# Second attention of a two-layer block: softmax weights turned one step later, ahead of the norm in VectorE's step

## The chip, the cores and the metric

One Trainium2 chip, one core. The metric is the device time of one execution in microseconds (us), the median of several runs. Engines: PE is TensorE, DVE is VectorE, ACT is ScalarE, POOL is GpSimd, and SP issues most of the DMAs.

## The reference

Two layers over x of shape (8, 512, 256), 4096 tokens of width 256. Each layer modulates a layer norm, adds a gated attention, norms again, and adds a gated mixture of experts. The change lies in the attention of the second layer, where each token attends over its own 16 heads, not over other tokens:

```python
h = _layernorm(x) * (1 + ca) + sa
Q, K, V = (x @ Wq.T), (x @ Wk.T), (x @ Wv.T)      # each reshaped to (b, s, 16 heads, 16)
scores = jnp.einsum('bshd,bstd->bsht', Q, K) / math.sqrt(hd)
attn = jax.nn.softmax(scores, axis=-1)            # 16 x 16 for every token
out = jnp.einsum('bsht,bstd->bshd', attn, V).reshape(b, s, dm)
x = x + ga * (out @ Wfc.T)
h = _layernorm(x) * (1 + cb) + sb                 # then the second layer's experts: logits = h @ Wg, ...
```

## The kernel before, in words

The kernel is written engine by engine, with explicit semaphores (`c_["name"]`, counted up by one for each tile). The second attention works on 32 tiles (NT) of 128 tokens; four tiles (TB) form a batch. It is a software pipeline: `tile_steps` runs a step counter s, and in step s every stage with lag LAG handles tile t = s - LAG, in the order of the list that the engine hands over. No scheduler moves anything: the list is the engine's program order, and an engine that waits holds up all that stands behind.

The way of one tile, with line, engine and lag before the change:

- L1576 PE turns the normed rows (2), ACT shifts them (L1502), L1585 PE makes values (3), L1509 ACT keeps them, SP stores and reloads them (L1342, L1352).
- L1596 PE makes queries and keys (6), L1515 ACT keeps them; after every fourth tile SP moves the keys with four DMAs (`turn_k`, L1361).
- L1652 PE `scores` (10), into PSUM banks 0 to 3, which are not doubled: the scores of a tile wait until ACT has copied those of the tile before (`compact`, L1523, semaphore `comp`).
- L1396 POOL `mask_other` (11), L1429 DVE `max_scores` (11), L1401 POOL `sub_max` (11), L1530 ACT `exps` (12), L1433 and L1434 DVE `sum_exp` (12), L1406 POOL `normalize_exp` (13), L1443 DVE `turn_exp` (13): four block transposes that turn the weights into `ebd`. All of them work in place on the buffer `sc`.
- L1631 PE `weigh` (14), L1536 ACT keeps the result. After every fourth tile L1607 PE `project` (15), into the same PSUM banks as the scores, and L1453 DVE `gate_attention` (15), for which the next scores wait.
- L1412 POOL `add_attention` (19), L1459 and L1460 DVE `stats_sum` (19), L1492 and L1494 ACT `rstd2` (19), L1469 and L1470 DVE `norm2` (20), L1616 PE `turn_h` (20), L1542 ACT `keep_h1T` (20), L1640 PE `logits` (20), L1546 ACT `keep_logits` (20).

Every fourth step is a step with a projection; PE and ACT use a second list in it. In ACT's ordinary list the copy of the scores is in two halves, and the second half, which alone counts `comp` up, stands behind `keep_h1T`; in the list of a step with a projection the whole copy stands first:

```python
tile_steps([(LAG_MX, compact((0, 1), False)), (LAG_N, shift_h), (LAG_V, keep_v), (LAG_EX, exps), (LAG_H, keep_h1T),
            (LAG_MX, compact((2, 3), True)), (LAG_QK, keep_qk), ...],
           [(LAG_MX, compact((0, 1, 2, 3), True)), ...])
```

The last four tiles' norms run after the loop (`LAST`), and in the two last steps with weights PE runs 12 filler matmuls (`hold_clock`, L277).

Of the kernel before, what the change touches and what calls it, by code (L numbers as in the profile page):

```python
# [61 lines left out]
def two_layer_kernel(nc, a):  # L62
    ctx = ExitStack()
    with ctx:
# [1203 lines left out]
        zqk = [cv(P * H).rearrange("p (t h) -> p t h", h=H) for _ in range(2)]  # L1268
        zk = [cv(P * H).rearrange("p (t h) -> p t h", h=H) for _ in range(2)]
        ebd = [cv(GR * P).rearrange("p (g n) -> p g n", g=GR) for _ in range(2)]  # L1270
        sc = [cv(GR * 32).rearrange("p (g n) -> p g n", n=32) for _ in range(3)]
        oT = cv(HH * P).rearrange("p (j t) -> p j t", j=HH)
        h1 = [rows[:, i * D:(i + 1) * D] for i in range(2 + TB)]
        yb = cv(TB * D).rearrange("p (k d) -> p k d", d=D)
# [24 lines left out]
        v_d = nc.dram_tensor("v_turn", [NT, P, D], F32).ap()  # L1299

        LAG_N, LAG_V, LAG_VST, LAG_QK, LAG_VLD, LAG_S = 2, 3, 4, 6, 7, 10
        LAG_MX, LAG_EX, LAG_ET, LAG_PV, LAG_Y = 11, 12, 13, 14, 15
        LAG_XLD, LAG_ROW, LAG_X, LAG_H = 14, 16, 19, 20

        def tile_steps(stages, project_steps=None):

# [19 lines left out]
        with nc.Block() as block:  # L1326
# [59 lines left out]
            @block.gpsimd  # L1386
            def _(eng):
                attn0_gpsimd(eng)
                f0_gpsimd(eng)
                eng.memset(ebd[0], 0.0)  # L1390
                eng.memset(ebd[1], 0.0).then_inc(s_ebz, 1)

                def mask_other(t):
                    eng.wait_ge(c_["comp"], t + 1)
                    s3 = sc[t % 3]
                    eng.tensor_tensor(s3, s3, bc_mid(pair_mask, GR), ALU.add).then_inc(c_["msk"], 1)  # L1396

                def sub_max(t):
                    eng.wait_ge(c_["mx"], t + 1)
                    s3 = sc[t % 3]  # L1400
                    eng.tensor_tensor(s3, s3, bc_last(mx1[t % 2], 32), ALU.subtract).then_inc(c_["sub"], 1)  # L1401

                def normalize_exp(t):
                    eng.wait_ge(c_["sm"], t + 1)
                    s3 = sc[t % 3]
                    eng.tensor_tensor(s3, s3, bc_last(rs1[t % 2], 32), ALU.mult).then_inc(c_["mul"], 1)  # L1406

                def add_attention(t):
                    b, k = t // TB, t % TB
                    eng.wait_ge(c_["ya"], b + 1)  # L1410
                    eng.wait_ge(s_x1[b % 2], 16 * (b // 2 + 1))
                    eng.tensor_tensor(xr[b % 3][:, k, :], xr[b % 3][:, k, :], yb[:, k, :], ALU.add).then_inc(c_["xa"], 1)  # L1412
                tile_steps([(LAG_ET, normalize_exp), (LAG_X, add_attention), (LAG_MX, mask_other), (LAG_MX, sub_max)])
                for t in LAST:
                    add_attention(t)

            @block.vector
            def _(eng):
                attn0_vector(eng)
                plan0_vector(eng)  # L1420
                f0_vector(eng)
                ch = Chain(eng, "s_vc")
                for v in vp[0:2]:
                    eng.memset(v, 0.0)
                eng.memset(vp[2], 0.0).then_inc(s_vz, 1)

                def max_scores(t):
                    eng.wait_ge(c_["msk"], t + 1)
                    eng.tensor_reduce(mx1[t % 2], sc[t % 3], AX.X, ALU.max).then_inc(c_["mx"], 1)  # L1429

                def sum_exp(t):
                    eng.wait_ge(c_["ex"], t + 1)
                    ch.do(eng.tensor_reduce(rs1[t % 2], sc[t % 3], AX.X, ALU.add))  # L1433
                    eng.reciprocal(rs1[t % 2], rs1[t % 2]).then_inc(c_["sm"], 1)  # L1434

                def turn_exp(t):
                    eng.wait_ge(c_["mul"], t + 1)
                    if t < 2:
                        eng.wait_ge(s_ebz, 1)
                    wait_some(eng, c_["pv"], t - 1)  # L1440
                    for q in range(4):
                        rows_q = slice(32 * q, 32 * q + 32)
                        last = eng.transpose(ebd[t % 2][rows_q, :, 32 * q:32 * q + 32], sc[t % 3][rows_q])  # L1443
                    last.then_inc(c_["et"], 1)

                def gate_attention(t):
                    b = t // TB
                    if t % TB == TB - 1:
                        eng.wait_ge(c_["y"], b + 1)
                        eng.wait_ge(s_m3[b % 2], 48 * (b // 2 + 1))  # L1450
                        wait_some(eng, c_["xa"], TB * b)
                        for k in range(TB):
                            last = eng.tensor_tensor(yb[:, k, :], b_y[k], mod3[b % 2][:, 0, :], ALU.mult)  # L1453
                        last.then_inc(c_["ya"], 1)

                def stats_sum(t):
                    eng.wait_ge(c_["xa"], t + 1)
                    ln = one_of(ln2, t)
                    ch.do(eng.bn_stats(ln[0], xr[t // TB % 3][:, t % TB, :]))  # L1459
                    eng.bn_aggr(ln[1], ln[0]).then_inc(c_["mv2"], 1)  # L1460

                def norm2(t):
                    m3 = mod3[t // TB % 2]
                    h, (_, mean, rstd) = one_of(h1, t), one_of(ln2, t)
                    eng.wait_ge(c_["rs2"], t + 1)
                    if t < FIRST_LAST:
                        wait_some(eng, c_["tH"], t - 1)
                        wait_some(eng, s_hst[t % 2], t // 2, 16)
                    ch.do(eng.scalar_tensor_tensor(h, xr[t // TB % 3][:, t % TB, :], mean[:, 0:1], m3[:, 1, :], ALU.subtract, ALU.mult))  # L1469
                    eng.scalar_tensor_tensor(h, h, rstd, m3[:, 2, :], ALU.mult, ALU.add).then_inc(c_["h"], 1)  # L1470
                tile_steps([(LAG_H, norm2), (LAG_ET, turn_exp), (LAG_X, stats_sum), (LAG_MX, max_scores), (LAG_EX, sum_exp),
                            (LAG_Y, gate_attention)])
                norm2(FIRST_LAST - 1)
                stats_sum(FIRST_LAST)
                for t in LAST:
                    if t + 1 < NT:
                        stats_sum(t + 1)
                    norm2(t)

            @block.scalar  # L1480
            def _(eng):
# [35 lines left out]
                def compact(quads, done):  # L1517
                    def stage(t):
                        eng.wait_ge(c_["ss"], t + 1)
                        wait_some(eng, c_["et"], t - 2)  # L1520
                        for q in quads:
                            rows_q = slice(32 * q, 32 * q + 32)
                            last = eng.activation(sc[t % 3][rows_q], b_s[rows_q, :, 32 * q:32 * q + 32], ACT.Copy)  # L1523
                        if done:
                            last.then_inc(c_["comp"], 1)
                    return stage

                def exps(t):
                    eng.wait_ge(c_["sub"], t + 1)
                    eng.activation(sc[t % 3], sc[t % 3], ACT.Exp, scale=HD ** -0.5).then_inc(c_["ex"], 1)  # L1530

                def keep_oT(t):
                    p = t % TB
# [334 lines left out]
```

## Time and profile before

| | before |
|---|---|
| median of 3 runs | 1058.15 us (1058.12 to 1059.05) |
| the profiled execution's own time | 1056.94 us |
| its span, first to last instruction | 1055.1 us |
| PE busy | 966.2 us (92%) |
| DVE busy | 621.1 us (59%) |
| ACT busy | 493.6 us (47%) |
| POOL busy | 384.3 us (36%) |
| second attention, first scores to the last logits | 555.8 to 830 us of the span |

The shares are averages over stages with different limits. The second attention takes a quarter of the span, and what a change in it is worth has to be read in its own steps. The granted clock of TensorE has two levels here, 1.00 (2.4 GHz) and 0.50 (1.2 GHz).

### The profile page before, as it was taken

Reading aid. Unit: us, or ns where it says so; the run is one execution under the profiler, and the core shown is the slowest. Engines: PE = TensorE matmul, PEld = TensorE weight load, DVE = VectorE, ACT = ScalarE, POOL = GpSimd, SP = SyncE. Lnnn points to the kernel's source line nnn. Section 1 sums busy time; section 2 is a strip of 40 time slices with the busy share of each in tenths; the row PEclk is TensorE's granted clock in tenths of the full one; section 3 lists DMA queues with packets and bytes.
Section 4 is the critical chain, followed back from the end, with each engine's and each line's share of the span. In section 5 each row is a group of like instructions: output and inputs, shape, how many; then the busy total and the mean of one; then the engine's idle time right before and its main releaser. Section 6 shows DMA issues by size and latency. Waiting matters only on the chain. (4 is left out here: it accounts for less than half of the span.)

```text
span 1055.1 us, 30102 instructions
## 1 busy us (share of the span) xinstructions
PE 966.2 (92%) x11221; PEld 829.3 (79%) x11222; DVE 621.1 (59%) x1446; ACT 493.6 (47%) x1343; POOL 384.3 (36%) x341
## 2 busy tenths in 40 slices
PE   6999999999999999999988999999767888999996
PEld 3466666988999999999966877777656878899995
DVE  3478877763544444444513788888885777344442
ACT  2656665304445445454346786776552440322221
POOL 0535344421222222321203565555552101455552
PEclk9999999899999999999998999999858999999999
DMA  9874471295222222231055755766421620444441
GB/s 336 252 295 122 123 260 46 93 355 149 87 90 90 83 95 88 76 98 60 8 117 83 131 123 138 149 136 124 87 73 55 250 122 20 151 133 139 133 135 35
DMA packets 133008, 135.58 MB, mean 128 GB/s; under 512 B 73868, under 2 KB 122126, under 8 KB 130724
## 3 DMA queue, kind: packets, MB, share of 16 engines
q1 hardware_dynamic: 121668, 90.80, 30.9%
q0 software_dynamic: 11232, 43.27, 12.9%
q8 instruction: 76, 1.25, 0.5%
q14 instruction: 32, 0.26, 0.1%
HBM read 96.21 MB, written 44.77 MB: 134 GB/s over the span
## 5 line engine op out<-in xcount | busy, mean ns | idle before, releaser
L1132 PE MATMUL psall<-rows 128*128 128x128 f32 x1872 | 221.9, 275 | 2.4 <-DVE rows L1186 2.4
L1132 PEld LDWEIGHTS psall<-rows 128*128 128x128 f32 x1872 | 215.3, 192 | 2.9 <-issue 2.8
L1099 POOL DMA_INDIRECT x<-ffn_rows,tok_i x78 | 82.7, 1060 | 242.1 <-DVE rows L1205 141.1
L1144 PE MATMUL psall<-whi,rows 128*128 x624 | 141.0, 379 | 0.0
L1186 DVE COPY rows<-wlo 128x2048 f32 (+1 forms) x78 | 74.9, 960 | 108.4 <-PE psall L1132 102.3
L1144 PEld LDWEIGHTS psall<-whi,rows 128*128 128x128 f32 x624 | 115.7, 190 | 14.1
L1443 DVE STREAM_TRANSPOSE whi<-whi 32x512 f32<-32x512 f32 x128 | 89.8, 701 | 9.0 <-POOL whi L1406 7.7
L277 PE MATMUL psall<-cst 128*128 128x128 f32 x722 | 91.8, 285 | 0.5 <-PEq L1326 0.5
L1523 ACT ACTIVATE whi<-psall 32x512 f32<-32x512 f32 x128 | 75.2, 587 | 30.4 <-PE psall L1652 25.7
L1245 ACT ACTIVATE rows<-psall,vs 128x128 f32<-128x128 f32 x312 | 84.9, 383 | 9.5 <-PE psall L1132 5.9
L277 PEld LDWEIGHTS psall<-cst 128*128 128x128 f32 x722 | 87.7, 200 | 0.7 <-issue 0.6
L1104 POOL DMA_INDIRECT attn_rows<-rows,tok_i x39 | 39.6, 1015 | 120.3 <-DVE rows L1218 120.3
L1396 POOL TENSOR_TENSOR whi<-whi,cst 128x512 f32<-128x512 f32 x32 | 40.7, 1271 | 92.5 <-ACT whi L1523 92.5
L1144 PE MATMUL psall<-wlo,rows 128*128 x312 | 73.6, 379 | 0.0
L1173 ACT ACTIVATE small<-small,eps_t 128x1 f32<-128x1 f32 x39 | 11.5, 295 | 116.5 <-DVE small L1213 116.5
L1596 PE MATMUL psall<-wlo,x 128*32 128x128 f32 x2048 | 63.5, 277 | 0.0
L1199 DVE TENSOR_TENSOR rows<-psall,x 128x256 f32<-128x256 f32 x39 | 16.6, 425 | 79.4 <-PE psall L1144 78.9
L1596 PEld LDWEIGHTS psall<-wlo,x 128*32 128x32 f32 x2048 | 54.8, 111 | 10.5 <-issue 9.3
L1144 PEld LDWEIGHTS psall<-wlo,rows 128*128 128x128 f32 x312 | 56.4, 190 | 6.1
L759 PE MATMUL psall<-whi 128*128 128x512 f32 x128 | 58.3, 598 | 2.1 <-ACT key L665 1.1
L1652 PE MATMUL psall<-whi 16*128 16x128 f32 x1024 | 42.0, 301 | 19.1 <-ACT whi L1523 8.2
L1429 DVE TENSOR_REDUCE wlo<-whi 128x16 f32<-128x512 f32 x32 | 21.8, 680 | 57.1 <-POOL whi L1396 56.3
(251 smaller groups left out, 1680.1 us busy)
## 6 DMA issues: line engine op xcount, KB each, us to landing
ffn_rows<-mod_rows SPq DMA_DIRECT2D x2, 4096.0 KB
wlo<-in_W SPq DMA_DIRECT2D x2, 4096.0 KB, 17.3
whi<-in_w SPq DMA_DIRECT2D x5, 1024.0 KB, 8.5
whi<-mod_rows SPq DMA_DIRECT2D x4, 1024.0 KB, 14.3
ffn_rows<-rows SPq DMA_DIRECT2D x8, 512.0 KB
ffn_rows<-x SPq DMA_DIRECT2D x8, 512.0 KB
wlo<-attn_rows SPq DMA_DIRECT2D x32, 128.0 KB, 3.6
v_turn<-wlo SPq DMA_DIRECT2D x32, 128.0 KB, 3.1
```

Of the source, the lines that this page charges most:

```text
L277: eng.matmul(b_idle, ident, ident, start=True, stop=True)
L759: last = eng.matmul(ps[k % 2][:, :], h0T[:, c, k * P:(k + 1) * P], wqkv[:, c, D:3 * D], start=c == 0, stop=c == C - 1)
L1099: eng.indirect_dma_start(xin[j % DEEP], None, src_d, bass.IndirectOffsetOnAxis(tok_i[:, j:j + 1].bitcast(U32), 0), bounds_check=T, oob_is_ ...
L1132: last = eng.matmul(b_up[t.par][f // 4][:, (f % 4) * P:(f % 4 + 1) * P], w_now[:, c, f * P:(f + 1) * P], inT[t.par][:, c * P:(c + 1) * P], ...
L1144: last = eng.matmul(b_dn[t.par][:, 0:D], hidT[t.par][:, f * P:(f + 1) * P], w_down[:, bass.ds(e, 1), f, :].rearrange("p o n -> p (o n)"), ...
L1186: eng.tensor_copy(w_now, w_up[:, bass.ds(e, 1)].rearrange("p o c n -> p (o c) n")).then_inc(e_["w"], 1)
L1245: last = eng.activation(dst[:, f * P:(f + 1) * P], banks[f // 4][:, (f % 4) * P:(f % 4 + 1) * P], ACT.Relu, bias=b1T[:, f, bass.ds(e, 1)])
L1396: eng.tensor_tensor(s3, s3, bc_mid(pair_mask, GR), ALU.add).then_inc(c_["msk"], 1)
L1443: last = eng.transpose(ebd[t % 2][rows_q, :, 32 * q:32 * q + 32], sc[t % 3][rows_q])
L1523: last = eng.activation(sc[t % 3][rows_q], b_s[rows_q, :, 32 * q:32 * q + 32], ACT.Copy)
L1596: last = eng.matmul(b_qk[t % 2][k * QD:(k + 1) * QD, n * P:(n + 1) * P], wqkv1[:, c, h * QD:(h + 1) * QD], hT[b % 2][:, c, k * P:(k + 1) * ...
L1652: last = eng.matmul(b_s[:, 4 * k + g, :], zqk[b % 2][at, tok, :].rearrange("p t h -> p (t h)"), zk[b % 2][at, tok, :].rearrange("p t h -> ...
```

## The change

The turned weights move one step later (lag 13 to 14) while their normalization stays (now named LAG_MUL, 13). On DVE the two first entries of the list change places: `turn_exp` is first, `norm2` second. `sc` gets a fourth buffer, and ACT's copy may run one tile further ahead. Weighing, projection, gate, the load of x, the rows of the modulation, sum, statistics, norm, turned rows and logits all get one step later, so that the loop has 48 steps instead of 47. The lists of PE, ACT, POOL and SP keep their order.

```diff
-        sc = [cv(GR * 32).rearrange("p (g n) -> p g n", n=32) for _ in range(3)]
+        sc = [cv(GR * 32).rearrange("p (g n) -> p g n", n=32) for _ in range(4)]
...
         LAG_N, LAG_V, LAG_VST, LAG_QK, LAG_VLD, LAG_S = 2, 3, 4, 6, 7, 10
-        LAG_MX, LAG_EX, LAG_ET, LAG_PV, LAG_Y = 11, 12, 13, 14, 15
-        LAG_XLD, LAG_ROW, LAG_X, LAG_H = 14, 16, 19, 20
+        LAG_MX, LAG_EX, LAG_MUL, LAG_ET, LAG_PV, LAG_Y = 11, 12, 13, 14, 15, 16
+        LAG_XLD, LAG_ROW, LAG_X, LAG_H = 15, 17, 20, 21
...
-                tile_steps([(LAG_ET, normalize_exp), (LAG_X, add_attention), (LAG_MX, mask_other), (LAG_MX, sub_max)])
+                tile_steps([(LAG_MUL, normalize_exp), (LAG_X, add_attention), (LAG_MX, mask_other), (LAG_MX, sub_max)])
...
-                tile_steps([(LAG_H, norm2), (LAG_ET, turn_exp), (LAG_X, stats_sum), (LAG_MX, max_scores), (LAG_EX, sum_exp),
+                tile_steps([(LAG_ET, turn_exp), (LAG_H, norm2), (LAG_X, stats_sum), (LAG_MX, max_scores), (LAG_EX, sum_exp),
                             (LAG_Y, gate_attention)])
...
                         eng.wait_ge(c_["ss"], t + 1)
-                        wait_some(eng, c_["et"], t - 2)
+                        wait_some(eng, c_["et"], t - 3)
```

Every other `t % 3` on `sc` becomes `t % 4`.

On VectorE, one ordinary step in the middle of the second attention stood like this before (norm of one tile, transposes, statistics of the sum, maximum, sum of exponentials and its reciprocal):

```order
L1469 SCALAR_TENSOR_TENSOR rows<-wlo,small 128x256
L1470 SCALAR_TENSOR_TENSOR rows<-rows,small,wlo 128x256
L1443 STREAM_TRANSPOSE whi<-whi 32x16x32 x4
L1459 BN_STATS small<-wlo 128x6
L1460 BN_AGGR small<-small 128x2
L1429 TENSOR_REDUCE wlo<-whi 128x16
L1433 TENSOR_REDUCE wlo<-whi 128x16
L1434 RECIPROCAL wlo<-wlo 128x16
```

And the same step on VectorE with the change:

```order
L1443 STREAM_TRANSPOSE whi<-whi 32x16x32 x4
L1469 SCALAR_TENSOR_TENSOR rows<-wlo,small 128x256
L1470 SCALAR_TENSOR_TENSOR rows<-rows,small,wlo 128x256
L1459 BN_STATS small<-wlo 128x6
L1460 BN_AGGR small<-small 128x2
L1429 TENSOR_REDUCE wlo<-whi 128x16
L1433 TENSOR_REDUCE wlo<-whi 128x16
L1434 RECIPROCAL wlo<-wlo 128x16
```

The four transposes no longer stand between the norm and the maximum; only the statistics do.

On ScalarE an ordinary step stands, before and with the change alike, as follows (first half of the copied scores, shifted rows, values, exponentials, the normed rows turned by TensorE, second half of the scores, queries and keys, weighed values, logits, and the two activations of the next norm's scale):

```order
L1523 ACTIVATE whi<-psall 32x512 x2
L1502 ACTIVATE wlo<-psall,modT 128x128 x2
L1509 ACTIVATE wlo<-psall 128x256
L1530 ACTIVATE whi<-whi 128x512
L1542 ACTIVATE wlo<-psall 128x256
L1523 ACTIVATE whi<-psall 32x512 x2
L1515 ACTIVATE whi<-psall 128x128x4
L1536 ACTIVATE whi<-psall 128x8x32
L1546 ACTIVATE key<-psall 128x8
L1492 ACTIVATE small<-small,eps_t 128x1
L1494 ACTIVATE small<-small 128x1
```

Nothing moved inside this step; L1542, which needs this step's norm, still stands ahead of the second L1523.

## Rows read from the trace of the kernel before

**Rows 1.** The page: busy time of the engines over the span.

```profile
PE 966.2 (92%) x11221; PEld 829.3 (79%) x11222; DVE 621.1 (59%) x1446; ACT 493.6 (47%) x1343; POOL 384.3 (36%) x341
```

**Rows 2.** Timeline of VectorE, one ordinary step: start, duration, [idle before].

```profile
683.27 0.69 DVE L1429 TENSOR_REDUCE wlo<-whi 128x16 f32<-128x512 f32 x1
...
684.75 0.61 DVE L1469 SCALAR_TENSOR_TENSOR rows<-wlo,small 128x256 f32<-128x256 f32 x1
...
685.40 1.15 DVE L1470 SCALAR_TENSOR_TENSOR rows<-rows,small,wlo 128x256 f32<-128x256 f32 x1
...
686.48 2.85 DVE L1443 STREAM_TRANSPOSE whi<-whi 32x512 f32<-32x512 f32 x4
...
689.35 0.43 DVE L1459 BATCH_NORM_STATS2 small<-wlo 128x6 f32<-128x256 f32 x1
...
690.07 0.69 DVE L1429 TENSOR_REDUCE wlo<-whi 128x16 f32<-128x512 f32 x1
```

**Rows 3.** Timeline of the other engines in the same step.

```profile
685.04 1.23 POOL L1406 TENSOR_TENSOR whi<-whi,wlo 128x512 f32<-128x512 f32 x1
...
686.61 0.44 PE L1616 MATMUL psall<-cst,rows 128*128 128x128 f32 x2 [0.17 <-DVE rows L1470]
...
687.09 0.39 ACT L1542 ACTIVATE wlo<-psall 128x256 f32<-128x256 f32 x1 [0.56 <-PE psall L1616]
687.49 1.19 ACT L1523 ACTIVATE whi<-psall 32x512 f32<-32x512 f32 x2
...
688.76 1.28 POOL L1396 TENSOR_TENSOR whi<-whi,cst 128x512 f32<-128x512 f32 x1 [1.62 <-ACT whi L1523]
...
688.94 1.17 PE L1652 MATMUL psall<-whi 16*128 16x128 f32 x32 [0.32 <-ACT whi L1523]
```

**Rows 4.** Timeline of VectorE: a gate, the maximum behind it, and a later one.

```profile
698.16 1.36 DVE L1453 TENSOR_TENSOR whi<-psall,wlo 128x256 f32<-128x256 f32 x4
...
707.35 0.69 DVE L1429 TENSOR_REDUCE wlo<-whi 128x16 f32<-128x512 f32 x1 [3.13 <-POOL whi L1396]
...
736.98 0.69 DVE L1429 TENSOR_REDUCE wlo<-whi 128x16 f32<-128x512 f32 x1 [1.88 <-POOL whi L1396]
```

**Rows 5.** Timeline of TensorE behind that gate.

```profile
699.67 1.17 PE L1652 MATMUL psall<-whi 16*128 16x128 f32 x32 [0.83 <-DVE whi L1453]
...
703.89 0.44 PE L1616 MATMUL psall<-cst,rows 128*128 128x128 f32 x2
```

**Rows 6.** Timeline of VectorE at the end of the second attention.

```profile
789.65 0.65 DVE L1429 TENSOR_REDUCE wlo<-whi 128x16 f32<-128x512 f32 x1
...
799.86 0.42 DVE L1469 SCALAR_TENSOR_TENSOR rows<-wlo,small 128x256 f32<-128x256 f32 x1
...
808.36 0.48 DVE L1469 SCALAR_TENSOR_TENSOR rows<-wlo,small 128x256 f32<-128x256 f32 x1 [3.44 <-ACT small L1494]
808.88 0.48 DVE L1470 SCALAR_TENSOR_TENSOR rows<-rows,small,wlo 128x256 f32<-128x256 f32 x1
```

**Rows 7.** Timeline of VectorE in a step ahead of the first norm.

```profile
578.32 2.85 DVE L1443 STREAM_TRANSPOSE whi<-whi 32x512 f32<-32x512 f32 x4 [1.29 <-POOL whi L1406]
```

**Rows 8.** Timeline of TensorE, scores of tiles 2, 3 and 4.

```profile
568.48 1.17 PE L1652 MATMUL psall<-whi 16*128 16x128 f32 x32 [1.11 <-ACT whi L1523]
...
573.87 1.17 PE L1652 MATMUL psall<-whi 16*128 16x128 f32 x32 [1.10 <-ACT whi L1523]
...
581.28 1.17 PE L1652 MATMUL psall<-whi 16*128 16x128 f32 x32 [1.01 <-issue]
```

**Rows 9.** Timeline of SP: the four key DMAs ahead of the scores of tile 4.

```profile
574.37 3.31 SPq L1361 DMA_DIRECT2D whi<-whi  x4
```

**Rows 10.** DMA issues of the stage: count, KB each, median us from issue to landing.

```profile
whi<-whi SPq DMA_DIRECT2D x28, 128.0 KB, 4.2
...
wlo<-mod_rows SPq DMA_DIRECT2D x24, 128.0 KB, 3.6
```

**Rows 11.** Timeline of TensorE: an early and a late projection.

```profile
723.91 3.74 PE L1607 MATMUL psall<-rows,whi 32*128 32x256 f32 x64
...
754.38 6.63 PE L1607 MATMUL psall<-rows,whi 32*128 32x256 f32 x64 [2.57 <-ACT whi L1523]
```

**Rows 12.** Windows: us, busy of PE, PEld, DVE, ACT, POOL, then the granted clock.

```profile
756.00:760.00 4.00, 4.00 (x43) 3.57 (x40) 2.64 (x6) 0.50 (x2) 2.05 (x2) 0.50 0.73 202
```

More of the change, by code:

```diff
@@ L1394, in mask_other @@
                     eng.wait_ge(c_["comp"], t + 1)
-                    s3 = sc[t % 3]
+                    s3 = sc[t % 4]
                     eng.tensor_tensor(s3, s3, bc_mid(pair_mask, GR), ALU.add).then_inc(c_["msk"], 1)
@@ L1399, in sub_max @@
                     eng.wait_ge(c_["mx"], t + 1)
-                    s3 = sc[t % 3]
+                    s3 = sc[t % 4]
                     eng.tensor_tensor(s3, s3, bc_last(mx1[t % 2], 32), ALU.subtract).then_inc(c_["sub"], 1)
@@ L1404, in normalize_exp @@
                     eng.wait_ge(c_["sm"], t + 1)
-                    s3 = sc[t % 3]
+                    s3 = sc[t % 4]
                     eng.tensor_tensor(s3, s3, bc_last(rs1[t % 2], 32), ALU.mult).then_inc(c_["mul"], 1)
@@ L1428, in max_scores @@
                     eng.wait_ge(c_["msk"], t + 1)
-                    eng.tensor_reduce(mx1[t % 2], sc[t % 3], AX.X, ALU.max).then_inc(c_["mx"], 1)
+                    eng.tensor_reduce(mx1[t % 2], sc[t % 4], AX.X, ALU.max).then_inc(c_["mx"], 1)
                 def sum_exp(t):
                     eng.wait_ge(c_["ex"], t + 1)
-                    ch.do(eng.tensor_reduce(rs1[t % 2], sc[t % 3], AX.X, ALU.add))
+                    ch.do(eng.tensor_reduce(rs1[t % 2], sc[t % 4], AX.X, ALU.add))
                     eng.reciprocal(rs1[t % 2], rs1[t % 2]).then_inc(c_["sm"], 1)
@@ L1442, in turn_exp @@
                         rows_q = slice(32 * q, 32 * q + 32)
-                        last = eng.transpose(ebd[t % 2][rows_q, :, 32 * q:32 * q + 32], sc[t % 3][rows_q])
+                        last = eng.transpose(ebd[t % 2][rows_q, :, 32 * q:32 * q + 32], sc[t % 4][rows_q])
                     last.then_inc(c_["et"], 1)
@@ L1519, in stage @@
                         eng.wait_ge(c_["ss"], t + 1)
-                        wait_some(eng, c_["et"], t - 2)
+                        wait_some(eng, c_["et"], t - 3)
                         for q in quads:
                             rows_q = slice(32 * q, 32 * q + 32)
-                            last = eng.activation(sc[t % 3][rows_q], b_s[rows_q, :, 32 * q:32 * q + 32], ACT.Copy)
+                            last = eng.activation(sc[t % 4][rows_q], b_s[rows_q, :, 32 * q:32 * q + 32], ACT.Copy)
                         if done:
@@ L1529, in exps @@
                     eng.wait_ge(c_["sub"], t + 1)
-                    eng.activation(sc[t % 3], sc[t % 3], ACT.Exp, scale=HD ** -0.5).then_inc(c_["ex"], 1)
+                    eng.activation(sc[t % 4], sc[t % 4], ACT.Exp, scale=HD ** -0.5).then_inc(c_["ex"], 1)
                 def keep_oT(t):
```

## The prediction

> **What bounds the kernel now.** The page comes first: PE is busy 92% of the span, the other engines about 59% or less [rows 1]. That says only that PE leads on average. The second attention is read in its own steps, on VectorE's timeline, since the change reorders VectorE.
>
> An ordinary step in the middle lasts from one maximum to the next, 690.07 - 683.27 = 6.80 us [rows 2]. VectorE shows no idle time in it at all. One might conclude that VectorE's load is the bound and that only its length matters. The timelines of the other engines say more [rows 3]. The norm's second half ends at 685.40 + 1.15 = 686.55. PE turns the rows at 686.61, ACT copies them at 687.09, and right behind that copy, at 687.49, stands the second half of the copied scores, which ends at 688.68. POOL masks them at 688.76 and ends at 690.04, and the maximum starts at 690.07. So there is a chain of 690.07 - 686.55 = 3.52 us, from the end of the norm to the maximum of the same step, through PE, ACT and POOL. VectorE's own work between the two, four transposes and the statistics, from 686.48 on, takes just as long, so the chain is exactly hidden and shows no wait. The reader should see that two paths tie here: transposes and statistics on VectorE, and the norm's chain outside it.
>
> The step behind a projection is different. There the maximum waits 3.13 us for the mask [rows 4], since the scores start only when the gate is done (699.67), and PE then goes through its list up to the turned rows at 703.89 without waiting [rows 5]. That step is set by PE, not by VectorE.
>
> **The change, part by part.** *Order on VectorE.* The transposes now come ahead of the norm. ACT's list is unchanged: the copy of the turned rows still stands ahead of the second half of the scores. So an ordinary step becomes a closed loop: maximum, sum and reciprocal (from 683.27 to 684.75, 1.48 us [rows 2]); transposes (686.48 to 689.35, 2.87 us [rows 2]); norm; and then the chain of 3.52 us, of which only the statistics lie on VectorE. For the norm I take it undisturbed. At the end of the stage it takes 808.88 + 0.48 - 808.36 = 1.00 us [rows 6], against 1.80 in the ordinary step, from 684.75 to 686.55, where POOL's normalization runs beside it [rows 3]. With the change POOL's normalization starts with the transposes and ends before the norm. The loop is 1.48 + 2.87 + 1.00 + 3.52 = 8.87 us instead of 6.80, so +2.07 us. The bounds of this cost: with the norm at its disturbed 1.80 it is 2.87, and below, if chain and handovers run 0.1 us shorter, 1.97. I take 2.07, because POOL's 1.23 us fits into 2.87 us of transposes.
>
> How many such steps? Norm and maximum are both active in steps 21 to 42 after the change. Those with a projection (23, 27, ... 39) copy all scores first in ACT's list and have no such chain; those behind one (24, 28, ... 40) keep PE's length: the transposes start with the end of the gate, 698.16 + 1.36 = 699.52, the norm ends 3.87 us later at 703.4, and PE wants it at 703.89 [rows 4, 5]. That leaves 21, 22, 25, 26, 29, 30, 33, 34, 37, 38, 41 and 42, twelve steps: 12 x 2.07 = **+24.8 us**.
>
> A rule of the Trainium skill bears on the norm. The row first: while POOL's normalization of 1.23 us runs [rows 3], the norm's two instructions take 0.61 and 1.15 us [rows 2], and 0.48 each when nothing runs on POOL [rows 6]. The page SBUF — State Buffer, section on the two sides of the memory, says that a VectorE instruction with two inputs from SBUF and a GpSimd instruction share one pair of ports, and that the one which starts first holds it until it ends. By that, the change takes 0.8 us off VectorE's step; what would follow from it alone is the first rival.
>
> *Late steps behind a projection.* When PE has nothing left of queries and values, the wait of the maximum is 1.88 us instead of 3.13 [rows 4], a step of 10.63 - 1.25 = 9.4. The new loop there is 1.48 + 1.3 for the gate + 2.87 + 1.00 + 3.52 = 10.2. Two such steps, +0.8 each, against steps into a projection that may get 0.2 shorter: **+0.5**.
>
> *Start.* Before the first norm, VectorE waits 1.29 us in every step for the normalization [rows 7], which now has a step's time; PE's step is 5.39 us (568.48 to 573.87 [rows 8]), so some 0.3 us each over seven steps is gained, 2 us. Against it: the scores of every fourth tile need the key DMAs. For tile 4 the interval is 581.28 - 573.87 = 7.41 us instead of 5.39 [rows 8]; the issues, from 574.37 on, take 3.31 us [rows 9], and each lands 4.2 us after its issue [rows 10], so the last one at about 581. Tile 8's scores stood in the step with the first projection, which gave them time; now they stand ahead of it and wait about 2 us as tile 4's do. In the same SP step the three DMAs of the modulation's rows now stand ahead of the key DMAs. Sum 0, between -2 and +4. In the middle, steps of 8.87 us leave the key DMAs, some 3.3 + 4.2 us, room.
>
> *End.* There is one more step behind the last maximum, and it holds a norm. Before, 799.86 - 789.65 = 10.21 us lie between the last maximum and the norm of tile 24, and 8.50 to the next [rows 6]. After, VectorE does maximum and sum (1.48), transposes (2.87), norm (1.00), statistics (0.72), sum (0.88), gate (1.3), transposes (2.87), norm (1.3), statistics (0.7), transposes (2.87): 16.0, so +5.8. Behind tile 24 the last transposes (2.85) are out of the way, which can give back up to 2; a wait on the last weighing can add 1. I take **+5**, between +3.5 and +7.
>
> *The fourth buffer.* The buffers of scores live one step longer and there is one more: nothing, and no gain, since no ACT wait on the transposes shows in the ordinary step. If it did not cover, the copy would wait for VectorE's transposes in the step before, which now come first: still nothing.
>
> *TensorE's clock.* In the ordinary step PE waits 0.17 + 0.32 us [rows 3] of 6.80, so its own work is 6.3 us; in the new step it waits 2.5 us, in one piece, ahead of the turned rows. After a wait of 2.57 us a projection took 6.63 us instead of 3.74 [rows 11], at a granted clock of 0.50, the 1.2 GHz level [rows 12]. Nothing if the clock holds; 2.9 us for each of five projections that now run fast but would not then, and up to 2 us for each of eight ordinary steps whose 6.3 us nearly double, at the other end. I take **+1**, near the lower end, because PE reaches queries and keys again in every step and a slow PE has 2.5 us of slack.
>
> Sum: 24.8 + 0.5 + 0 + 5 + 1 = +31.3 us on the profiled execution's own 1056.94, that is 1088.2. The median of the runs shown is 1.2 us above that execution, so 1089.4.
>
> **The rivals.** *Faster: VectorE's own load is the bound.* For it: VectorE has no idle time in the ordinary step, and loses 0.8 us of disturbed norm. Then the step falls to PE's 6.3 us, 17 ordinary steps x -0.5 = -8.5, with +5 at the end: 1058 - 3.5 = 1054.6. Against it: the chain of rows is real program order, and would have to be 2.57 us shorter to let this through (3.52 against statistics and handovers of 0.7, less the slack between 8.87 and 6.3). It decides only if ACT's copy of the scores did not stand behind the turned rows. Chance 3%. The skill's page SBUF — State Buffer points this way, since it prices the freed ports and nothing else.
>
> *No change.* Gains of the first kind and the longer end cancel: 1058. It needs the same break of the chain. 3%.
>
> *TensorE's clock falls in most of the new steps.* For it: the 2.57 us case. Against it: in the middle no row shows a slow clock. Price: about half of 5 x 2.9 + 8 x 2, 15 us: 1104. Chance 16%.
>
> *The key DMAs are late in the middle too.* SP has the modulation's rows (3 issues, each landing after 3.6 us [rows 10]) and the key DMAs in one step. If they come 1.5 us late in six batches: +9, 1098. Against it: 8.87 us against 7.5. Chance 5%.
>
> **How the numbers follow.** My forecast, the chain of 12 steps, has 73%: 1089, its own range 1081 to 1096. The range for 8 in 10 reaches over the DMA rival and most of the clock rival: 1080 to 1103. Below 0.2% a measurement of this kernel tells nothing from no change. Slower 0.94, same 0.03, faster 0.03.
>
> **What the profile after would show.** On VectorE, in two of four steps, the maximum idles about 2.8 us for POOL's mask, and PE's turned rows wait some 2.5 us for the norm; maxima 8.9 us apart there, and about 10.6 behind a projection as before. The norm's instructions at 0.5 us each. The first scores to the last logits about 31 us longer. The prediction is wrong if the maximum has no wait in those steps, or if PE's clock drops to 0.50 in the middle of the stage, or if the scores of every fourth tile wait for a DMA.

## The result: 3.5% slower

| | before | after |
|---|---|---|
| median of 4 runs each | 1058.13 us (1057.23 to 1059.05) | 1095.88 us (1094.79 to 1096.93) |
| ratio, 95% interval | | 1.0347 (1.0325 to 1.0370) |
| the profiled execution's own time, span | 1056.94, 1055.1 us | 1094.79, 1093.0 us |

The forecast was 1089 us with a range of 1080 to 1103, so the time lies inside, near the upper end; the loss was 37.8 us where 31.3 had been summed.

The page of the kernel after, the line that answers to [rows 1]:

```profile
PE 986.7 (90%) x11221; PEld 844.7 (77%) x11222; DVE 604.8 (55%) x1446; ACT 494.7 (45%) x1343; POOL 375.5 (34%) x341
```

VectorE and GpSimd do the same instructions in less busy time (604.8 against 621.1, 375.5 against 384.3). The norm and POOL's normalization no longer run side by side: the norm's two instructions take 0.49 and 0.48 us instead of 0.61 and 1.15 [rows 2], the normalization 1.05 instead of 1.23 [rows 3]. The kernel is slower all the same. An ordinary step shows why. VectorE's timeline of the kernel after, which answers to [rows 2], from one maximum to the third behind it:

```profile
659.75 0.69 DVE L1429 TENSOR_REDUCE wlo<-whi 128x16 f32<-128x512 f32 x1 [3.47 <-POOL whi L1396]
660.35 0.68 DVE L1433 TENSOR_REDUCE wlo<-whi 128x16 f32<-128x512 f32 x1
661.06 0.25 DVE L1434 RECIPROCAL wlo<-wlo 128x16 f32<-128x16 f32 x1
661.23 2.79 DVE L1443 STREAM_TRANSPOSE whi<-whi 32x512 f32<-32x512 f32 x4
664.05 0.49 DVE L1469 SCALAR_TENSOR_TENSOR rows<-wlo,small 128x256 f32<-128x256 f32 x1
664.58 0.48 DVE L1470 SCALAR_TENSOR_TENSOR rows<-rows,small,wlo 128x256 f32<-128x256 f32 x1
664.98 0.42 DVE L1459 BATCH_NORM_STATS2 small<-wlo 128x6 f32<-128x256 f32 x1
665.43 0.18 DVE L1460 BATCH_NORM_AGGREGATE small<-small 128x2 f32<-128x6 f32 x1
...
668.56 0.69 DVE L1429 TENSOR_REDUCE wlo<-whi 128x16 f32<-128x512 f32 x1 [2.95 <-POOL whi L1396]
...
677.83 0.69 DVE L1429 TENSOR_REDUCE wlo<-whi 128x16 f32<-128x512 f32 x1 [3.39 <-POOL whi L1396]
...
683.84 0.65 DVE L1429 TENSOR_REDUCE wlo<-whi 128x16 f32<-128x512 f32 x1
```

The step from 659.75 lasts 8.81 us instead of 6.80. The norm ends at 665.06, and then VectorE has only the statistics to do and waits 2.95 us for POOL's mask. The other engines in the same step, which answer to [rows 3]:

```profile
661.52 1.05 POOL L1406 TENSOR_TENSOR whi<-whi,wlo 128x512 f32<-128x512 f32 x1
...
665.12 0.44 PE L1616 MATMUL psall<-cst,rows 128*128 128x128 f32 x2 [2.20 <-DVE rows L1470]
...
665.59 0.38 ACT L1542 ACTIVATE wlo<-psall 128x256 f32<-128x256 f32 x1 [2.94 <-PE psall L1616]
666.00 1.19 ACT L1523 ACTIVATE whi<-psall 32x512 f32<-32x512 f32 x2
...
667.27 1.26 POOL L1396 TENSOR_TENSOR whi<-whi,cst 128x512 f32<-128x512 f32 x1 [4.02 <-ACT whi L1523]
```

Every link of the predicted chain stands there in order: norm, turned rows (PE has waited 2.20 us), their copy (ACT has waited 2.94), second half of the scores, mask, maximum; 668.56 - 665.06 = 3.50 us against 3.52 before. The last interval above, from 677.83 to 683.84, is a step into a projection, 6.01 us, where ACT copies all scores first: VectorE runs through it without a wait.

To see where the whole loss sits, the second attention is cut at the first maximum, that of tile 9, that of tile 31 and the last norm. VectorE's timelines, first of the kernel before, then of the kernel after:

```profile
563.28 0.69 DVE L1429 TENSOR_REDUCE wlo<-whi 128x16 f32<-128x512 f32 x1 [32.67 <-POOL whi L1396]
...
621.54 0.69 DVE L1429 TENSOR_REDUCE wlo<-whi 128x16 f32<-128x512 f32 x1
...
826.92 0.48 DVE L1469 SCALAR_TENSOR_TENSOR rows<-wlo,small 128x256 f32<-128x256 f32 x1
```

```profile
562.84 0.69 DVE L1429 TENSOR_REDUCE wlo<-whi 128x16 f32<-128x512 f32 x1 [31.21 <-POOL whi L1396]
...
625.01 0.69 DVE L1429 TENSOR_REDUCE wlo<-whi 128x16 f32<-128x512 f32 x1 [3.33 <-POOL whi L1396]
...
820.57 0.69 DVE L1429 TENSOR_REDUCE wlo<-whi 128x16 f32<-128x512 f32 x1 [3.20 <-POOL whi L1396]
...
864.76 0.48 DVE L1469 SCALAR_TENSOR_TENSOR rows<-wlo,small 128x256 f32<-128x256 f32 x1
```

Start 58.3 to 62.2 (+3.9), middle 168.1 to 195.6 (+27.5), end 37.3 to 44.2 (+6.9), with 789.65 of [rows 6] for the maximum of tile 31 before. The sum is 38.3 us, practically the whole loss.

By kind of step the 27.5 us of the middle divide as follows. It holds twelve ordinary steps after the change; at 8.82 us each they take 24.0 us more than the twelve steps that stood there before, and what some of them take beyond 8.82 adds 4.0. Five steps into a projection give back 2.5, and the five behind one cost 2.0, all of it in the last two.

### The profile page after: what moved, and what is told of

Its sections match the earlier page's. It is cut to its first block and busy times, and to the rows that moved or that the text cites. A ratio compares the mean times of both kernels' runs of the same rounds, so it can differ in the third digit from the quotient of the medians.

```text
span 1093.0 us, 30100 instructions
## 1 busy us (share of the span) xinstructions
PE 986.7 (90%) x11221; PEld 844.7 (77%) x11222; DVE 604.8 (55%) x1446; ACT 494.7 (45%) x1343; POOL 375.5 (34%) x341
## 5 line engine op out<-in xcount | busy, mean ns | idle before, releaser
L1523 ACT ACTIVATE whi<-psall 32x512 f32<-32x512 f32 x128 | 75.2, 588 | 35.7 <-PE psall L1652 33.4
L277 PE MATMUL psall<-cst 128*128 128x128 f32 x722 | 89.6, 281 | 0.5 <-PEq L1326 0.5
L1596 PEld LDWEIGHTS psall<-wlo,x 128*32 128x32 f32 x2048 | 58.4, 117 | 13.0 <-issue 9.9
L1596 PE MATMUL psall<-wlo,x 128*32 128x128 f32 x2048 | 67.7, 288 | 0.0
L1652 PE MATMUL psall<-whi 16*128 16x128 f32 x1024 | 46.2, 328 | 16.4 <-DMA whi<-whi 9.3
L759 PE MATMUL psall<-whi 128*128 128x512 f32 x128 | 58.3, 598 | 1.5 <-ACT key L665 1.1
```

The lines of the kernel that those rows point to most:

```text
L277: eng.matmul(b_idle, ident, ident, start=True, stop=True)
L759: last = eng.matmul(ps[k % 2][:, :], h0T[:, c, k * P:(k + 1) * P], wqkv[:, c, D:3 * D], start=c == 0, stop=c == C - 1)
L1523: last = eng.activation(sc[t % 4][rows_q], b_s[rows_q, :, 32 * q:32 * q + 32], ACT.Copy)
L1596: last = eng.matmul(b_qk[t % 2][k * QD:(k + 1) * QD, n * P:(n + 1) * P], wqkv1[:, c, h * QD:(h + 1) * QD], hT[b % 2][:, c, k * P:(k + 1) * ...
L1652: last = eng.matmul(b_s[:, 4 * k + g, :], zqk[b % 2][at, tok, :].rearrange("p t h -> p (t h)"), zk[b % 2][at, tok, :].rearrange("p t h -> ...
```

## Experiments

The theory, as the prediction had it: with the transposes ahead of the norm, norm, turned rows, their copy, second half of the scores, mask and maximum close a loop with the transposes. The rivals: the later lags make the loss; TensorE's clock does; TensorE's own wait for the turned rows does. The three stretches, measured between the same marks in each profile, in us; the median of the timed runs; and its ratio to runs of the kernel before that were taken beside it (their medians are 1058.1 to 1061.3 us). The stretches are those of one execution each, and its own time can lie below the median: 1069.4 against 1074.9 us with the norm first again, 1074.0 against 1077.9 with the rows copied later.

| kernel | start | middle | end | median | ratio to before, 95% |
|---|---|---|---|---|---|
| before | 58.3 | 168.1 | 37.3 | | |
| after | 62.2 | 195.6 | 44.2 | 1095.9 | 1.0325 to 1.0370 |
| norm first again, new lags | 64.5 | 170.8 | 40.5 | 1074.9 | 1.0119 to 1.0188 |
| transposes first, old lags | 62.5 | 214.9 | 40.6 | 1115.0 | 1.0496 to 1.0566 |
| after, rows copied later | 62.2 | 174.6 | 45.2 | 1077.9 | 1.0151 to 1.0230 |
| after, whole copy first | 59.6 | 168.0 | 44.3 | 1065.2 | 1.0031 to 1.0071 |
| after, start filled | 63.0 | 198.0 | 44.2 | 1098.3 | 1.0315 to 1.0404 |
| after, all filled | 61.9 | 203.4 | 44.2 | 1105.0 | 1.0383 to 1.0480 |
| after, half filled | 62.1 | 190.8 | 46.7 | 1093.5 | 1.0271 to 1.0354 |
| after, three buffers | 79.8 | 233.7 | 44.2 | 1151.3 | 1.0800 to 1.0898 |
| before, whole copy first | 60.1 | 164.1 | 37.7 | 1053.1 | 0.9905 to 0.9945 |
| before, rows copied later | 58.1 | 161.0 | 38.0 | 1052.1 | 0.9895 to 0.9949 |
| before, scores ahead of exponentials | 56.5 | 158.9 | 38.0 | 1048.7 | 0.9897 to 0.9929 |

**Norm first again, all else as changed.**

```diff
-                tile_steps([(LAG_ET, turn_exp), (LAG_H, norm2), ...
+                tile_steps([(LAG_H, norm2), (LAG_ET, turn_exp), ...
```

> The changed kernel with VectorE's list turned back (norm first, transposes second); all lags, the fourth buffer and the early normalization stay. Theory (the chain from the norm through the turned rows, ACT's copy of them, the second half of the scores and the mask closes a loop with the transposes): ordinary steps fall from 8.82 back to 6.80 us, since transposes and statistics cover the chain again; 12 x 2.0 = 24 us and some slow-clock steps come back, the start (+4) and the end (+5 to +7) stay: 1066 us, between 1063 and 1071. Rival (the longer pipeline, the key DMAs or TensorE's clock make most of the loss): 1085 or more, the maxima still 8 us or more apart.

Measured: 1074.9 us. The middle falls by 24.7 us, and its ordinary steps are back at 6.8 us, as the theory said. VectorE's timeline of this kernel:

```profile
659.15 0.69 DVE L1429 TENSOR_REDUCE wlo<-whi 128x16 f32<-128x512 f32 x1 [3.27 <-POOL whi L1396]
...
665.95 0.69 DVE L1429 TENSOR_REDUCE wlo<-whi 128x16 f32<-128x512 f32 x1
...
672.74 0.69 DVE L1429 TENSOR_REDUCE wlo<-whi 128x16 f32<-128x512 f32 x1
```

But the time is 4 us above the bound that I gave. The profiled execution, 1069.4 us, is inside the range and the lowest of four that spread to 1077.0; what made the others longer no profile shows. Against the kernel before it lost 6.2 us in the start, 2.7 in the middle and 3.2 at the end, so the new lags, with the fourth buffer, cost some 1.5% alone. Part of that is the key DMAs, on TensorE's timeline of this kernel:

```profile
583.59 1.17 PE L1652 MATMUL psall<-whi 16*128 16x128 f32 x32 [3.40 <-DMA whi<-whi]
...
705.10 1.17 PE L1652 MATMUL psall<-whi 16*128 16x128 f32 x32 [1.28 <-DMA whi<-whi]
```

The scores of tiles 4 and 8 wait 3.40 and 2.37 us for them, longer than in the changed kernel, and those of tiles 12, 16, 20 and 24 wait 0.57 to 1.28 us. In the changed kernel none in the middle waits for a DMA.

**The order alone, on the kernel before.**

```diff
-                tile_steps([(LAG_H, norm2), (LAG_ET, turn_exp), ...
+                tile_steps([(LAG_ET, turn_exp), (LAG_H, norm2), ...
```

> The kernel before with nothing but the two entries of VectorE's list exchanged (transposes first, norm second), all lags as before. Theory: the same loop, and the normalization on POOL, which before ran beside the norm, joins it: 1.48 + 1.29 (VectorE's wait for the normalization in the steps ahead of the first norm) + 2.87 + 1.0 + 3.52 = 10.2 us for an ordinary step against 6.80; 12 x 3.4 = 41, a little more in the steps into a projection, no longer start: 1100 to 1112 us. Rival (the lags cost, not the order): within 5 us of 1058.

Measured: 1115.0 us, 3 us above the upper bound. Ordinary steps take 10.25 us (10.2 were expected). On VectorE's timeline the maximum waits 2.95 us for the mask as in the changed kernel, and the transposes wait 1.29 us for the normalization.

```profile
659.24 2.85 DVE L1443 STREAM_TRANSPOSE whi<-whi 32x512 f32<-32x512 f32 x4 [1.29 <-POOL whi L1406]
...
666.88 0.69 DVE L1429 TENSOR_REDUCE wlo<-whi 128x16 f32<-128x512 f32 x1 [3.20 <-POOL whi L1396]
...
677.13 0.69 DVE L1429 TENSOR_REDUCE wlo<-whi 128x16 f32<-128x512 f32 x1 [2.95 <-POOL whi L1396]
```

The order alone costs 46.8 us in the middle at the old lags, 24.7 at the new. So within the change the separated normalization does save something; the order is the bad part.

**The changed kernel, rows copied behind the scores on ScalarE.** VectorE's order stays as changed; only ACT's list is different:

```diff
-... (LAG_EX, exps), (LAG_H, keep_h1T), (LAG_MX, compact((2, 3), True)), (LAG_QK, keep_qk), ...
+... (LAG_EX, exps), (LAG_MX, compact((2, 3), True)), (LAG_H, keep_h1T), (LAG_QK, keep_qk), ...
```

> The changed kernel with keep_h1T behind the second half of the copied scores in ACT's ordinary list; VectorE's order stays as changed. Theory: the norm no longer stands between the scores and the mask; VectorE's wait for the mask in ordinary steps goes from 2.95 us to under 1, and steps to 6.3 to 7.2 us; start and end stay long: 1060 to 1072 us. Rival (what holds the step is PE, which waits for the norm's rows, wherever ACT copies the scores): steps stay above 8 us, 1085 or more.

Measured: 1077.9 us, 6 us above the range. The mechanism holds: 21.0 of the 27.5 us of the middle come back without any change on VectorE. The size was missed. VectorE's timeline:

```profile
690.12 0.69 DVE L1429 TENSOR_REDUCE wlo<-whi 128x16 f32<-128x512 f32 x1 [2.52 <-POOL whi L1396]
...
696.60 0.69 DVE L1429 TENSOR_REDUCE wlo<-whi 128x16 f32<-128x512 f32 x1 [0.61 <-POOL whi L1396]
```

Steps of 6.48 us stand beside ones of 7.46 us, and single ones of 8.79 and 10.71 us. The granted clock was 1.00 in the steps of 6.48 and 7.46, and 0.53 and 0.52 on average in the two long ones. What makes the 7.46 was not separated.

**The whole copy of the scores first, on either kernel.**

```diff
-(LAG_MX, compact((0, 1), False)), (LAG_N, shift_h), (LAG_V, keep_v), (LAG_EX, exps), (LAG_H, keep_h1T),
-(LAG_MX, compact((2, 3), True)), (LAG_QK, keep_qk), ...
+(LAG_MX, compact((0, 1, 2, 3), True)), (LAG_N, shift_h), (LAG_V, keep_v), (LAG_EX, exps), (LAG_H, keep_h1T),
+(LAG_QK, keep_qk), ...
```

On the kernel before:

> The kernel before with the whole copy of the scores first in ACT's ordinary list, as it already stands in the list of the steps with a projection; nothing else. Theory: the mask comes early in every step; the ordinary step stays at VectorE's own 6.8 us, but behind a projection the wait of 3.13 us for the mask falls below 1: about 2 us in each of six such steps, 1045 to 1053 us. Rival (shifted rows and values come later from ACT and hold PE): 1058 or more.

Measured: 1053.1 us, ratio 0.9925, at the edge of the range. Behind a projection the step falls in most places (from 10.63 to 9.05 and 8.70 us, but one is 11.63), and most of the other steps fall to 6.61, where the theory had left them at 6.8; the one that follows a step behind a projection grows, to some 7.3. On the changed kernel:

> The changed kernel with the whole copy of the scores first in ACT's ordinary list. Theory: the mask depends on no norm in any step; VectorE's load without the disturbed norm, 6.0 us, and TensorE's 6.3 us are what is left, so ordinary steps of 6.3 to 6.6 us, behind a projection about 9; M 9 to 31 in 158 to 165 us against 195.6; start and end stay 4 and 7 us long: 1055 to 1063 us. Rival (the later transposes hold the step by themselves): steps of 8 us or more.

Measured: 1065.2 us, 2 us above the range. VectorE's timeline of the changed kernel with the whole copy first:

```profile
658.25 0.69 DVE L1429 TENSOR_REDUCE wlo<-whi 128x16 f32<-128x512 f32 x1 [0.61 <-POOL whi L1396]
...
664.73 0.69 DVE L1429 TENSOR_REDUCE wlo<-whi 128x16 f32<-128x512 f32 x1 [0.61 <-POOL whi L1396]
...
671.21 0.69 DVE L1429 TENSOR_REDUCE wlo<-whi 128x16 f32<-128x512 f32 x1 [0.61 <-POOL whi L1396]
```

Ordinary steps take 6.48 us, shorter than the 6.80 of the kernel before, with VectorE's order as changed. So the transposes ahead of the norm hurt only through the chain. The middle, 168.0 us, is yet no shorter than before, and 3 us above what I had expected: steps near its end take up to 8.95 and 12.06 us, at a mean granted clock of 0.50 and 0.78. The start (+1.4) and end (+7.0) leave it slower than the kernel before.

**Filler matmuls for the clock.** In the changed kernel TensorE's clock fell behind several waits. Its windows: us, busy, then the granted clock.

```profile
584.00:588.00 4.00, 4.00 (x81) 0.58 0.94 228
608.00:612.00 4.00, 4.00 (x54) 0.60 0.69 124
...
700.00:704.00 4.00, 4.00 (x84) 0.50 0.35 86
```

The first two stand behind the waits for the key DMAs of tiles 4 and 8, the third behind a 2.20 us wait for the norm. The experiments run `hold_clock` there, results unused. In `scores` the waits for `comp` and `ya` move ahead of those for the keys, so that the fillers can stand between:

```diff
 def scores(t):                       # behind the waits for comp and ya, ahead of those for the keys
+    if t in (4, 8):
+        hold_clock(eng, 16 if t == 4 else 10, ps[0][:, 0:P])
```

> The changed kernel with filler matmuls (16 and 10, result unused) on TensorE where the scores of tiles 4 and 8 wait for their key DMAs (2.83 and 1.88 us). Theory: the waits stay, but the granted clock no longer falls behind them; the interval of the maxima of tiles 4 to 5 goes from 8.36 to about 5.4 us, that of 8 to 9 from 12.34 to 10.6: 4 to 5 us less than the changed kernel, 1091 us. Rival (the start is longer by the DMA waits themselves): the same time as the changed kernel, 1095 to 1097.

Measured: 1098.3 us. The fillers were twice as long as meant: TensorE's timeline shows 32 matmuls for a count of 16.

```profile
580.07 3.84 PE L277 MATMUL psall<-cst 128*128 128x128 f32 x32 [1.01 <-ACT whi L1523]
```

The time is above both expectations, and the start took 63.0 us, 0.9 longer. The granted clock did stay at 1.00 behind both waits, but the fillers of tile 4 end 1.8 us after the scores had started in the changed kernel, so what the clock is worth there doesn't follow. The middle, where nothing was edited, took 198.0 us against 195.6: so much it differs between two executions. The second kernel adds the twelve ordinary steps:

```diff
 def turn_h(t):
+    s = t + LAG_H
+    if s < 43 and s % 4 in (1, 2):
+        kept = min(s - LAG_QK, NT)
+        eng.wait_ge(c_["qke"], kept)
+        hold_clock(eng, 14 if s < 34 else 22 if s < 38 else 30, b_qk[(kept - 1) % 2][:, 0:P])
```

> As the kernel with a filled start, and filler matmuls (14 to 30) also ahead of the turned rows in the twelve ordinary steps, where TensorE waits 2.2 to 4.4 us for the norm. Theory (the loop is held by the chain through VectorE, ACT and POOL, and the clock only adds to it): all twelve ordinary steps at 8.8 us, the projections of 6.15 and 6.66 us at 3.74, together 7 to 8 us less than with the start alone: 1080 to 1085. Rival (the wait in the new steps is TensorE's own, at a low clock): steps fall well below 8.8. Rival (the clock's part is small): 1089 or more.

Measured: 1105.0 us, slower. The count of 14 was 28 matmuls, some 3.3 us, and with TensorE's own 6.3 us of the step that is more than the loop: the ordinary step grew from 8.82 to 9.52. It tells little of the clock; it agrees with some 6.2 us of TensorE's own work in a step (9.52 less the fillers), well below the loop. The third kernel has half of every count (8 and 5; 7, 11 and 15):

> As the kernel filled everywhere, with half the filler matmuls: each call had run twice as many matmuls as its count, 3.84 us where 2.83 were to be covered, so that the fillers themselves were late. Now 16 and 10 in front of the scores of tiles 4 and 8, 14, 22 or 30 ahead of the turned rows of the twelve ordinary steps (1.6 to 3.5 us). Theory (the clock only adds to the loop): ordinary steps all at 8.8 us, start and projections at the high clock: 5 to 9 us less than the changed kernel, 1087 to 1091 us. Rival (the clock's part is nil or the fillers can't hold it): 1095 or more.

Measured: 1093.5 us, between the two expectations; its interval reaches down to the changed kernel's ratio, so the gain rests on the stretches rather than on the median. VectorE's timeline and TensorE's window of it:

```profile
660.03 0.69 DVE L1429 TENSOR_REDUCE wlo<-whi 128x16 f32<-128x512 f32 x1 [3.43 <-POOL whi L1396]
...
668.85 0.69 DVE L1429 TENSOR_REDUCE wlo<-whi 128x16 f32<-128x512 f32 x1 [2.95 <-POOL whi L1396]
```

```profile
700.00:704.00 4.00, 3.88 (x107) 1.00 0.45 100
```

Eleven of the twelve ordinary steps take 8.82 to 8.84 us, and the wait of 2.95 us for the mask stays: that is the loop by itself. The twelfth, 10.78 us, stands near the end, where the granted clock was at 0.50 again in spite of the fillers (796 to 800 us). The middle is 4.8 us shorter than the changed kernel's; that much of the low clock's cost there the fillers took back. The start did not change (62.1), but it is no clean test: at tile 8 the fillers left a wait of 1.27 us, and the clock behind it fell to 0.60. The end took 2.5 us more.

**Three buffers.**

```diff
-        sc = [... for _ in range(4)]
+        sc = [... for _ in range(3)]
...
-                        wait_some(eng, c_["et"], t - 3)
+                        wait_some(eng, c_["et"], t - 2)
```

Every `t % 4` on `sc` is `t % 3` again.

> The changed kernel with three buffers of scores as before, ACT's copy waiting for the transposes of the tile three back, which now stand in the same step. The prediction said that the fourth buffer is worth nothing. Theory by the rows: in an ordinary step the second half of the copy comes after the norm anyway, so 8.8 us stay; in a step into a projection the whole copy (2.4 us) would start behind VectorE's transposes and end 2 us later: 6.01 becomes about 8, over five or six such steps and some at the start, 1105 to 1112 us. Rival (the prediction's sentence: no cover is needed): 1095 to 1097.

Measured: 1151.3 us, far above both. Waits of ACT, 620 to 800 us of this kernel's span:

```profile
ACT whi L1523 <- DVE whi L1443: 65.7, 17, 4.8
```

(us in total, times, longest.)

Even the first half of the copy waits for the transposes, up to 4.8 us, and shifted rows, values and exponentials stand behind it on ACT. An ordinary step takes 10.03 to 10.41 us (9.2 near the end) where 8.8 were expected; one into a projection takes 8.14, as expected; and the start takes 79.8 us.

**Before, rows copied later; before, scores ahead of the exponentials.** The tie of the kernel before can be loosened without touching VectorE. The first has the edit of the rows on the kernel before:

> The kernel before with keep_h1T behind the second half of the copied scores in ACT's ordinary list. Theory: in the kernel before, chain and VectorE's own work tie at 6.80 us, so taking the chain away gains nothing in ordinary steps, and about 0.5 to 1 us in the steps behind a projection, where the copied rows no longer stand ahead: 1053 to 1058 us. Rival (the chain alone sets the 6.80): ordinary steps fall to 6.3 us, 1048 or less.

Measured: 1052.1 us, just below the range. The step behind a projection falls from 10.63 to 9.57 us, and the ordinary one, of which the theory expected nothing, to 6.62. VectorE's timeline of it:

```profile
675.65 0.69 DVE L1429 TENSOR_REDUCE wlo<-whi 128x16 f32<-128x512 f32 x1 [2.06 <-POOL whi L1396]
...
682.29 0.65 DVE L1429 TENSOR_REDUCE wlo<-whi 128x16 f32<-128x512 f32 x1
...
688.90 0.65 DVE L1429 TENSOR_REDUCE wlo<-whi 128x16 f32<-128x512 f32 x1
```

So 6.61 to 6.64 us is VectorE's own load, and the tie of the kernel before was not exact: the chain set its 6.80 us, by 0.2. The second goes further:

```diff
-... (LAG_V, keep_v), (LAG_EX, exps), (LAG_H, keep_h1T), (LAG_MX, compact((2, 3), True)), (LAG_QK, keep_qk), ...
+... (LAG_V, keep_v), (LAG_MX, compact((2, 3), True)), (LAG_EX, exps), (LAG_H, keep_h1T), (LAG_QK, keep_qk), ...
```

> The kernel before with the second half of the copied scores ahead of the exponentials and of keep_h1T in ACT's ordinary list. With the second half just behind the exponentials (experiment with the rows later) the step behind a projection fell from 10.63 to 9.58 us and the ordinary one to 6.62, VectorE's own load. Theory: the mask comes another 0.6 us earlier behind a projection, 9.0 us there in seven places, nothing in ordinary steps: 1046 to 1051 us. Rival (the exponentials then come late for VectorE's sum, or rows and values late for TensorE): 1052 or more.

Measured: 1048.7 us, ratio 0.9913. VectorE's timeline of it:

```profile
662.87 0.65 DVE L1429 TENSOR_REDUCE wlo<-whi 128x16 f32<-128x512 f32 x1
...
672.01 0.69 DVE L1429 TENSOR_REDUCE wlo<-whi 128x16 f32<-128x512 f32 x1 [1.63 <-POOL whi L1396]
678.65 0.65 DVE L1429 TENSOR_REDUCE wlo<-whi 128x16 f32<-128x512 f32 x1
685.26 0.65 DVE L1429 TENSOR_REDUCE wlo<-whi 128x16 f32<-128x512 f32 x1
```

9.14 us behind a projection, 6.61 to 6.64 otherwise. This beats the kernel before by 0.9% and the changed one; the three versions of the kernel before with another ScalarE list are not told apart by their intervals.

## Why the prediction was right, step by step

**The loop: right, in mechanism and size.** The prediction said 8.87 us for an ordinary step, twelve of them, +24.8 us. Measured: 8.82 us at the high clock, twelve of them, +24.0. That turning the order back returns 24.7 us of the middle, almost the number forecast, is in part luck: in the ordinary steps 27.6 us come back, the slow clock's share with them, and 2.9 us are lost again in the steps into and behind a projection. Two kernels show the mechanism from two sides: one takes the order away, the other takes the link on ACT away and leaves the order (21.0 us back). The rival that TensorE's own wait holds the step fell with the half-filled kernel, where most of that wait is filled and the step is still 8.82 us.

One reading was off by a little: the prediction called the chain "exactly hidden". VectorE's timeline of the kernel before, the second half of the statistics:

```profile
689.82 0.18 DVE L1460 BATCH_NORM_AGGREGATE small<-small 128x2 f32<-128x6 f32 x1
```

It ended at 690.00 us and the mask at 690.04 [rows 3], and with the chain loosened the step is 6.62 us; so the chain already set the 6.80. It changes the forecast by nothing, since the +2.07 was counted from the measured 6.80.

**The first rival fell, but its premise was right.** VectorE's own step did shrink. The norm's two instructions take 0.49 and 0.48 us, and the step into a projection, where nothing waits, is 6.01 us against 6.64 before. The two experiments on the order show that the order does it and not the lags: with the norm first again it takes 0.61 and 1.15 us beside the normalization, with the transposes first at the old lags 0.48 and 0.48. That agrees with the Trainium skill, page SBUF — State Buffer, section "SBUF: two separate sides": with POOL's normalization moved away from the norm, the shared pair of ports is free for it. In the steps that wait, the shorter norm is a link of the loop: with it at 1.80 us the step would be about 9.6 us instead of 8.82 (an estimate, from the 0.79 us by which it got shorter). So it softened the loss and did not prevent it. The prediction put 0.2 us on the step into a projection; it was 0.63.

**Steps behind and into a projection: +0.5 predicted, -0.5 measured.** The first of the two late steps went about as worked out, from 9.40 to 10.12 us; the second went from 11.74 to 13.01. The steps into a projection, 2.5 us less in all, made good more than that.

**The start: the term was 0, it measured +3.9 us.** The key DMAs of tile 8 do hold its scores, and tile 4's wait became one piece. TensorE's timeline of the kernel after, which answers to [rows 8]:

```profile
582.10 1.17 PE L1652 MATMUL psall<-whi 16*128 16x128 f32 x32 [2.83 <-DMA whi<-whi]
...
607.24 1.61 PE L1652 MATMUL psall<-whi 16*128 16x128 f32 x32 [1.88 <-DMA whi<-whi]
```

Before, weighing stood between two waits of 1.00 and 1.01 us ahead of tile 4's scores, and the clock held. The gain of 0.3 us a step was there in three of the seven steps (5.39 instead of 5.74). From the maximum of tile 3 to that of tile 5 it took 1.4 us longer, from that of tile 7 to that of tile 9 1.8, and from the first maximum to the second 1.5, which the prediction had not looked at: there TensorE's queries and keys stood at a granted clock of 0.57 where they had 0.71 (560 to 564 us). How the 3.9 us divide between DMA and clock stays open; the fillers did not settle it. The prediction's last sentence named scores of every fourth tile that wait for a DMA as a sign of being wrong: it came for tiles 4 and 8 in the start, and for none in the middle.

**The end: +5 predicted, +6.9 measured.** Up to 2 us were to be given back behind tile 24. VectorE's timeline at the end, which answers to [rows 6]:

```profile
834.66 2.85 DVE L1443 STREAM_TRANSPOSE whi<-whi 32x512 f32<-32x512 f32 x4 [1.72 <-PE psall L1631]
837.55 0.48 DVE L1469 SCALAR_TENSOR_TENSOR rows<-wlo,small 128x256 f32<-128x256 f32 x1
...
846.20 0.48 DVE L1469 SCALAR_TENSOR_TENSOR rows<-wlo,small 128x256 f32<-128x256 f32 x1 [7.09 <-ACT small L1494]
```

From the last maximum to tile 24's norm it took 16.98 us against 10.21, so nearly the whole loss of the end is there. VectorE's own work in it was 15.3 us, 0.7 less than the 16.0 summed, and the wait on weighing 1.72 where up to 1 was allowed. To the next norm it took 8.65 us against 8.50: nothing was given back, because that norm waits for ACT (3.44 us before [rows 6], 7.09 now), not for the transposes. The experiments with one half of the change each take 40.5 and 40.6 us at the end: order and lags share the loss.

**The clock: +1 predicted, some 4 to 5 us measured in the middle.** The ordinary steps took 4.0 us beyond 8.82 each, and fillers took back 4.8. "A slow PE has 2.5 us of slack" holds for most steps, where the loss is 0.2 to 0.5 us, but one step took 10.70 us. And the prediction had set the fall of the clock against a wait of 2.57 us; it fell behind waits of 2.20 us too. By the prediction's own last sentence, a clock of 0.50 in the middle was one of the things that would make it wrong; it did come, and cost a third of what the rival had priced. That sign was also badly chosen, and "in the middle no row shows a slow clock" was wrong: the late middle of the kernel before, from about 754 us on, was mostly at that level already, in [rows 12] and in this window (busy of PE, then the granted clock):

```profile
776.00:780.00 4.00, 2.50 (x38) 0.50 0.00 0
```

**The sum.** The time is inside the range because the largest term, the loop, was right. Start, end and clock were each too small, by 3.9, 1.9 and some 3 us, and the loop and the steps around the projections made up for only 1.8 of it: 1095.9 is the very edge of the forecast's own 1081 to 1096.

**The fourth buffer: the sentence was wrong.** "If it did not cover ... still nothing" missed by 55 us. It placed the transposes that the copy would wait for "in the step before". With three buffers at the new lags they are those of the same step: the copy of tile t waits for the transposes of tile t - 3, and both handle their tile in step t + 11. So even the first half of the copy is late, and with it all that follows on ACT.

## What to carry to other kernels

An engine without idle time in a step need not be the bound: follow the results that leave it and come back within the step, and compare that chain with the work that covers it. Here they tied within 0.2 us, and moving the cover away cost 2.0 us in each of twelve steps, although no instruction of VectorE in the step got slower. When such a tie is found, the link to move is the one that does not belong to the chain (a copy that stands ahead of another on a third engine); that took 0.8 to 0.9% off, by one entry of a list.

## What the runs showed of the hardware that was not expected

TensorE's granted clock fell to 0.50 behind waits of only 2.20 us for the norm, with the turned rows, weighing and logits right behind them (700 to 704 us of the changed kernel); the same stretch with 1.83 us of fillers in the wait, which left 0.64 us of it, kept it at 1.00. A call for one f32 128x128 filler matmul appears as two in the trace: 32 matmuls and 3.84 us for a count of 16.
